# Cross-attention on one Trainium2 core: row maxima subtracted on VectorE, probabilities summed on GpSimd

## The chip, the cores and the metric

The kernel is one program on 1 core of a Trainium2 chip. The metric is the device time of that core in microseconds (us), from launch to the last result. Engines are named as the profile names them: PE is TensorE, DVE is VectorE, ACT is ScalarE, POOL is GpSimd, SP is SyncE. SBUF is the on-chip memory, PSUM the accumulators that PE writes.

## The reference

Three layers run one after the other: cross-attention, a mixer (attention on a quarter of the tokens, a state-space scan on the rest) and an expert layer. Only cross-attention is touched. Cut to it:

```python
def cross_attention(x1, x2, Wq1, Wk1, Wv1, Wk2, Wv2, Wo, bo):   # B=4, N1=256, N2=4096, D=256, 8 heads of 64
    q1, k1, v1 = heads(x1 @ Wq1), heads(x1 @ Wk1), heads(x1 @ Wv1)
    k2, v2 = heads(x2 @ Wk2), heads(x2 @ Wv2)
    k, v = concat([k1, k2], axis=1), concat([v1, v2], axis=1)    # 4352 keys
    sim = einsum('bihd,bjhd->bhij', q1, k) * 64 ** -0.5
    attn = softmax(sim, axis=-1)
    return einsum('bhij,bjhd->bihd', attn, v).reshape(B, N1, 512) @ Wo + bo
x = x + cross_attention(layernorm(x), ctx_1024, ...)
```

## The kernel before, in words

**Units, steps, tiles.** The work of cross-attention is cut into 16 units `u`: 4 batches, and in each 4 pairs of heads. A unit scores its 256 queries against 4352 keys, which are 17 tiles `j` of 256 keys (`HG` = 17), each for both heads of the pair: 128 partitions x 1024 numbers. The keys come in 9 groups `g` (`NG` = 9). A unit has 9 steps `d`: step `d` scores the tiles 2d and 2d+1, step 8 tile 16 alone.

**Two units at once.** While unit `u` makes its probabilities, the next one, `v` = u+1, projects its keys and finds the maxima of its rows. Each engine has its own program in a fixed order, written out by hand, and an instruction waits on counters (semaphores) of the others. In a step in the middle of a unit:

- PE (`block.tensor`): `score_for_max(v, d-1, 1)`, `score(u, 2d)`, `score(u, 2d+1)`, `score_for_max(v, d, 0)`, `project_keys(v, d+1)`, `weigh(u, 2d-2)`, then the projections of values that are due (`v_due`), `weigh(u, 2d-1)`.
- ACT (`block.scalar`): `exponentials(u, 2d)`, `exponentials(u, 2d+1)`, `store_k_hi(v, d+1)`, then `store_values` of what is due and pieces of the splitting of context and weights.
- DVE (`block.vector`): `reduce_max(v, d-1, 1)`, `add_probs(u, 2d-1)`, `reduce_max(v, d, 0)`, `add_probs(u, 2d)`, `split_keys(v, d+1)`.
- POOL (`block.gpsimd`): only the low halves of context and weights (`split_chunk`, `split_query_weights`, `split_weights`, `split_values_weights`).

Projections of values are due in odd units from step 2 on (two tiles a step) and in the steps 0 and 1 of even units (three tiles). The steps 2 to 7 of even units, and the steps 0 and 1 of odd units, have none: they are called light here. Others are called heavy.

**How a score becomes a probability.** `score` (L760 to L775) makes four products for each quarter tile, both heads in pairs that run side by side in the two halves of the array: three of them are q times k in high and low parts, the fourth (L774) adds the negated row maximum, as ones times `neg_max`. So the scores lie shifted in one of two slots of PSUM (`S`). `exponentials` (L460) takes them from PSUM to `probs` in SBUF, a ring of four tiles (`RING` = 4); that frees the slot, which `score` waits for. `add_probs` (L548) adds the tile to `prob_sum`, and `weigh` (L777) multiplies it with the values into the bank `O`. At the end of a unit `sum_probs` (L790) sums `prob_sum` over the partitions, `invert_sums` and `normalize` divide.

**The maxima.** `score_for_max` scores v with the high parts alone, into `M`, a single buffer of two banks; `reduce_max` (L534) takes the maxima of it, and the next `score_for_max` waits for that. At the end of a unit `reduce_rows` puts them into `max_cols`, `turn_maxima` (L745) turns them over the partitions on PE, and `store_neg_max` (L544) stores them; `score(v, 0)` waits for it.

**The keys.** `project_keys` fills the bank `KQ`; ACT rounds it to `k_hi` (`store_k_hi`, L446), then DVE takes what is left to `k_lo` (`split_keys`, L525), which waits for `k_hi_done`.

After the last unit, which has no unit beside it, the mixer begins once the output is added to `X1`.

Of the kernel before, what the change touches and what calls it, by code (L numbers as in the profile page):

```python
# [9 lines left out]
ALU = mybir.AluOpType  # L10
# [132 lines left out]
def cross_attention(nc, x, ctxT, w, X1, ident, psum):  # L143
# [3 lines left out]
    with ctx:  # L147
# [36 lines left out]
        maxes = sb("xa_maxes", [P, QT, 2, NG])  # L184

        max_cols = sb("xa_max_cols", [P, QT, P])
        neg_max = sb("xa_neg_max", [P, N1], F32R)
# [41 lines left out]
        neg_max_ready = sem("xa_neg_max_ready")  # L229
# [120 lines left out]
        def _(pool):  # L350
            pool.memset(ident[:, :], 0.0).then_inc(setup, 1)
            pool.memset(ones[:, :].bitcast(F32), 1.0).then_inc(setup, 1)
            pool.memset(max_cols[:, :, :], 0.0).then_inc(setup, 1)
            pool.wait_ge(setup, 3)
# [27 lines left out]

            split_query_weights(0)
# [24 lines left out]
        def _(act):  # L408
# [105 lines left out]
        def _(dve):  # L514
# [25 lines left out]
            def reduce_rows(v):  # L540
                dve.wait_ge(max_reduced, (v + 1) * NG * QT)
                dve.tensor_reduce(max_cols[:, :, 0:P:HD], maxes[:, :, :, :], AX_X, ALU.max).then_inc(rowmax_done, 1)
# [5 lines left out]
            def add_probs(u, j):  # L548
                n = u * HG + j
                dve.wait_ge(exp_done, n + 1)  # L550
                if j == 1:
                    if u > 0:
                        dve.wait_ge(sums_ready, u)
                    dve.tensor_tensor(prob_sum[:, :], probs[:, (n - 1) % RING, :], probs[:, n % RING, :],
                                      ALU.add).then_inc(summed, 1)
                else:
                    dve.wait_ge(summed, sums_done(n) - 1)
                    dve.tensor_tensor(prob_sum[:, :], prob_sum[:, :], probs[:, n % RING, :],  # L558
# [2153 lines left out]
```

## Time and profile before

| what | value |
|---|---|
| median of 3 runs | 1659.54 us (1658.64 to 1662.66) |
| profiled execution | 1661.31 us, with a span of 1659.3 us from its first to its last instruction |
| PE busy | 1489.4 us, 90% |
| DVE busy | 1124.6 us, 68% |
| ACT busy | 712.1 us, 43% |
| POOL busy | 443.8 us, 27% |
| cross-attention | from the start to about 1160 us |

Busy time is the time in which an engine executed at least one instruction. Matmuls overlap each other in PE's pipeline: the profile models their ends, so what a matmul occupies is read from the distance between two starts, not from its duration. In the timelines below a row is: start in us, duration in us, engine, line, operation, output<-inputs, shapes, count, and in brackets how long the engine sat idle before it and what ended that. Rows with a count over 1 are merged instructions. The clock (PEclk) is what was granted to TensorE, 1.00 being 2.4 GHz and 0.50 being 1.2 GHz.

### The profile page before, as it was taken

The page shows a single profiled execution, that of the slowest core. Times are in us where ns is not written, and L with a number is a line of the kernel's source. Part 1 is how long each engine was busy: PE and PEld are TensorE (multiplying, and loading weights), DVE is VectorE, ACT ScalarE, POOL GpSimd, SP SyncE. Part 2 cuts the span into 40 slices and gives each one's busy share as a digit, 9 for nine tenths or more (in the row PEclk, how much of TensorE's full clock was granted, in tenths as well). Part 3 has the DMA queues.
Part 4 walks back from the last instruction along what each step waited for, and adds up shares of the span by engine and source line. Part 5 has one row for each costly group of instructions (what it writes and reads, how often), then busy time and mean ns, then how long its engine had stood idle before and what let it go on. Part 6 is the DMA issues. An engine that isn't in the chain of part 4 may idle for free. (4 is left out here: it accounts for less than half of the span.)

```text
span 1659.3 us, 29603 instructions
## 1 busy us (share of the span) xinstructions
PE 1489.4 (90%) x11988; PEld 1121.4 (68%) x11988; DVE 1124.6 (68%) x1283; ACT 712.1 (43%) x971; POOL 443.8 (27%) x286
## 2 busy tenths in 40 slices
PE   4999999999999999999999999998597777827995
PEld 4877777776777777777777777766354444527995
DVE  2687578657657765865876685685676999644663
ACT  3443345443444543444454444333345333224773
POOL 4300003200000320100131000000133999433885
PEclk8999999999999999999999999999797999958998
DMA  5000021000002100000300000000304900092333
GB/s 174 14 11 11 1 84 51 1 14 11 11 15 87 36 2 14 20 1 27 99 11 2 23 11 2 2 1 1 84 10 178 231 0 0 1 362 63 63 59 58
DMA packets 62388, 76.50 MB, mean 46 GB/s; under 512 B 6385, under 2 KB 47985, under 8 KB 61857
## 3 DMA queue, kind: packets, MB, share of 16 engines
q1 hardware_dynamic: 57168, 68.51, 13.6%
q0 software_dynamic: 5088, 6.11, 2.5%
q8 instruction: 99, 1.62, 0.4%
q14 instruction: 33, 0.26, 0.1%
HBM read 58.39 MB, written 17.25 MB: 46 GB/s over the span
## 5 line engine op out<-in xcount | busy, mean ns | idle before, releaser
L537 DVE TENSOR_REDUCE xa_maxes<-psum 128x2 f32<-128x1024 f32 (+1 forms) x288 | 334.2, 1162 | 265.0 <-PE psum L741 264.9
L467 ACT ACTIVATE xa_probs<-psum 128x1024 f32<-128x1024 f32 x272 | 268.7, 1026 | 273.2 <-PE psum L774 272.8
L558 DVE TENSOR_TENSOR xa_prob_sum<-xa_prob_sum,xa_probs 128x1024 f32<-128x1024 f32 x240 | 313.1, 1305 | 11.3 <-ACT xa_probs L467 10.5
L786 PE MATMUL psum<-xa_probs,xa_vals 128*64 128x256 f32 x2176 | 280.5, 389 | 2.0 <-DVE xa_heads_T L572 1.5
L786 PEld LDWEIGHTS psum<-xa_probs,xa_vals 128*64 128x64 f32 x2176 | 139.4, 136 | 104.6 <-issue 41.8
L458 ACT ACTIVATE xa_vals<-psum 128x512 f32<-128x512 f32 x136 | 81.2, 597 | 207.6 <-PE psum L666 207.6
L768 PE MATMUL psum<-xa_q_hi,xa_k_hi 64*128 64x256 f32 x1088 | 156.4, 283 | 0.6 <-issue 0.6
L666 PE MATMUL psum<-xa_wv_hi,xa_ctx_hi 128*128 128x256 f32 x512 | 150.7, 294 | 4.4 <-DVE xa_maxes L537 4.4
L772 PE MATMUL psum<-xa_q_hi,xa_k_lo 64*128 64x256 f32 x1088 | 154.3, 279 | 0.0
L774 PE MATMUL psum<-xa_neg_max,xa_ones 64*128 64x256 f32 x1088 | 154.2, 279 | 0.0
L770 PE MATMUL psum<-xa_q_lo,xa_k_hi 64*128 64x256 f32 x1088 | 153.8, 278 | 0.0
L666 PE MATMUL psum<-xa_wv_lo,xa_ctx_hi 128*128 128x256 f32 x512 | 144.9, 283 | 0.0
L666 PE MATMUL psum<-xa_wv_hi,xa_ctx_lo 128*128 128x256 f32 x512 | 144.6, 283 | 0.0
L741 PE MATMUL psum<-xa_k_hi,xa_q_hi 64*128 64x512 f32 (+1 forms) x604 | 128.0, 430 | 15.2 <-DVE xa_maxes L537 8.7
L449 ACT ACTIVATE xa_k_hi<-psum 128x512 fp32r<-128x512 f32 (+1 forms) x151 | 83.0, 554 | 127.8 <-PE psum L666 127.8
L529 DVE TENSOR_TENSOR xa_k_lo<-psum,xa_k_hi 128x512 fp32r<-128x512 f32 (+1 forms) x151 | 94.5, 630 | 37.6 <-ACT xa_k_hi L449 37.3
L367 POOL TENSOR_TENSOR xa_w_lo<-xa_stage,xa_w_hi 128x512 fp32r<-128x512 f32 x16 | 20.5, 1282 | 371.9 <-ACT xa_w_hi L414 371.9
L361 POOL TENSOR_TENSOR xa_ctx_lo<-xa_ctx_in,xa_ctx_hi 128x1024 fp32r<-128x1024 f32 x32 | 79.6, 2491 | 145.8 <-ACT xa_ctx_hi L440 145.8
L666 PE MATMUL psum<-xa_ctx_hi,xa_w_hi 128*128 128x512 f32 x256 | 115.3, 450 | 2.5 <-issue 2.5
L666 PEld LDWEIGHTS psum<-xa_wv_hi,xa_ctx_hi 128*128 128x128 f32 x512 | 97.9, 191 | 27.3 <-issue 26.9
L1787 DVE TENSOR_TENSOR_SCAN mx_drive<-psum,mx_drive 128x768 f32<-128x768 f32 x64 | 110.0, 1743 | 7.8 <-POOL mx_drive L1312 6.9
L1312 POOL TENSOR_TENSOR mx_drive<-mx_xi,mx_rows 128x768 f32<-128x768 f32 x62 | 110.7, 1812 | 0.1
(329 smaller groups left out, 3019.5 us busy)
## 6 DMA issues: line engine op xcount, KB each, us to landing
xa_ctx_in<-in_ctxT_dram SPq DMA_DIRECT2D x32, 512.0 KB, 3.8
ex_slots<-mx_blank_tile SPq DMA_DIRECT2D x2, 4372.5 KB, 37.5
xa_stage<-in_L_xattn_Wk_dram SPq DMA_DIRECT2D x32, 128.0 KB, 2.4
xa_stage<-in_L_xattn_Wv_dram SPq DMA_DIRECT2D x16, 256.0 KB, 3.1
ex_raw<-in_L_ffn_w_gate_dram SPq DMA_DIRECT2D x8, 512.0 KB, 10.1
ex_raw<-in_L_ffn_w_up_dram SPq DMA_DIRECT2D x8, 512.0 KB, 10.8
ex_raw<-in_L_ffn_w_down_dram SPq DMA_DIRECT2D x8, 512.0 KB, 11.6
ex_xt<-ex_slots SPq DMA_DIRECT2D x15, 265.0 KB, 2.8
```

Of the source, the lines that this page charges most:

```text
L467: nc.scalar.activation(probs[:, n % RING, :], S[:, 2 * (n % 2):2 * (n % 2) + 2, :].rearrange("p h q -> p (h q)"), ACT.Exp, scale=HD ** -0. ...
L537: dve.tensor_reduce(maxes[:, qt, :, g:g + 1], max_banks(v, g, qt)[:, :, 0:group_keys(g)[1]], AX_X, ALU.max).then_inc(max_reduced, 1)
L558: dve.tensor_tensor(prob_sum[:, :], prob_sum[:, :], probs[:, n % RING, :], ALU.add).then_inc(summed, 1)
L666: i = pe.matmul(out, l, r, start=(c == 0 and k == 0), stop=(c == n - 1 and k == 2))
L741: i = pe.matmul(max_banks(v, g, qt)[:, h, part * N1:(part + slots) * N1], q_hi[half[h], v % 2, qt * P:(qt + 1) * P], k_hi[half[h], at:at + ...
L768: pe.matmul(out[h], k[h], q[h], start=True, stop=False)
L770: pe.matmul(out[h], k[h], q[2 + h], start=False, stop=False)
L772: pe.matmul(out[h], k[2 + h], q[h], start=False, stop=False)
L774: i = pe.matmul(out[h], ones[half[h], :], neg_max[half[h], :], start=False, stop=True)
L786: i = pe.matmul(O[half[h], 0:N1], vals[:, 2 * j + t, lanes:lanes + HD], probs[:, n % RING, (2 * h + t) * N1:(2 * h + t + 1) * N1], start=( ...
L1312: pool.tensor_tensor(drive[n % RINGS][:, :], dx[:, ct, :], b_rows[:, s, :], ALU.mult).then_inc(drive_done, 1)
L1787: dve.tensor_tensor_scan(drive[n % RINGS][:, :], decay[n % DECAYS], drive[n % RINGS][:, :], 0.0, ALU.mult, ALU.add).then_inc(scanned, 1)
```

## The change

The fourth product of `score` goes, and `neg_max` with it. The turned maxima are stored as they are, for both heads in all 128 partitions (`max_rows`, `store_max`), for which `turn_maxima` makes four turns of a broadcast column where it made two. DVE subtracts them from the scores on their way from PSUM to `probs` (`shift`), and that frees the slot of PSUM. ACT takes the exponential in place, from SBUF to SBUF, once `shifted` says so. `add_probs` is moved from DVE to POOL. The projection of the queries moves ahead of the last `weigh` of a unit. The order of ACT's program stays.

```diff
@@ block.gpsimd
+            def add_probs(u, j):
+                n = u * HG + j
+                pool.wait_ge(exp_done, n + 1)
+                if j == 1:
+                    if u > 0:
+                        pool.wait_ge(sums_ready, u)
+                    pool.tensor_tensor(prob_sum[:, :], probs[:, (n - 1) % RING, :], probs[:, n % RING, :],
+                                       ALU.add).then_inc(summed, 1)
+                else:
+                    pool.wait_ge(summed, sums_done(n) - 1)
+                    pool.tensor_tensor(prob_sum[:, :], prob_sum[:, :], probs[:, n % RING, :],
+                                       ALU.add).then_inc(summed, 1)
             for u, d in steps():
+                if d >= 1:
+                    add_probs(u, 2 * d - 1)
+                    add_probs(u, 2 * d)
@@ block.scalar
             def exponentials(u, j):
                 n = u * HG + j
-                if n >= RING:
-                    act.wait_ge(pv_done, n - RING + 1)
-                    act.wait_ge(summed, sums_done(n - RING))
-                act.wait_ge(scores_ready, n + 1)
-                nc.scalar.activation(probs[:, n % RING, :], S[:, 2 * (n % 2):2 * (n % 2) + 2, :].rearrange(
-                    "p h q -> p (h q)"), ACT.Exp, scale=HD ** -0.5).then_inc(exp_done, 1)
+                act.wait_ge(shifted, n + 1)
+                nc.scalar.activation(probs[:, n % RING, :], probs[:, n % RING, :], ACT.Exp,
+                                     scale=HD ** -0.5).then_inc(exp_done, 1)
@@ block.vector
-            def store_neg_max(v):
+            def store_max(v):
                 dve.wait_ge(max_turned, v + 1)
-                dve.tensor_scalar(neg_max[:, :], M[:, 1, 0:N1], -1.0, None, ALU.mult).then_inc(neg_max_ready, 1)
+                if v > 0:
+                    dve.wait_ge(shifted, v * HG)
+                dve.tensor_copy(max_rows[:, :, :].rearrange("p h q -> p (h q)"), M[:, 1, :]).then_inc(max_ready, 1)
+
+            def shift(u, j):
+
                 n = u * HG + j
+                dve.wait_ge(scores_ready, n + 1)
+                if j == 0:
+                    dve.wait_ge(max_ready, u + 1)
+                if n >= RING:
+                    dve.wait_ge(pv_done, n - RING + 1)
+                    dve.wait_ge(summed, sums_done(n - RING))
+                dve.tensor_tensor(probs[:, n % RING, :].rearrange("p (h t q) -> p h t q", h=2, t=2),
+                                  S[:, 2 * (n % 2):2 * (n % 2) + 2, :].rearrange("p h (t q) -> p h t q", t=2),
+                                  max_rows[:, :, :].unsqueeze(2).broadcast_to([P, 2, 2, N1]),
+                                  ALU.subtract).then_inc(shifted, 1)
@@ block.vector, the steps
-                if d >= 2 and not (d == STEPS - 1 and v < U):
-                    add_probs(u, 2 * d - 1)
+                shift(u, 2 * d)
                 if v < U:
                     reduce_max(v, d, 0)
                 if d < STEPS - 1:
-                    add_probs(u, 2 * d)
+                    shift(u, 2 * d + 1)
                     if v < U:
                         split_keys(v, d + 1)
@@ block.tensor
             def score(u, j):
                 n, g = u * HG + j, (j + 1) // 2
                 if n >= 2:
-                    pe.wait_ge(exp_done, n - 1)
-                if j == 0:
-                    pe.wait_ge(neg_max_ready, u + 1)
+                    pe.wait_ge(shifted, n - 1)
                     for h in range(2):
-                        pe.matmul(out[h], k[2 + h], q[h], start=False, stop=False)
-                    for h in range(2):
-                        i = pe.matmul(out[h], ones[half[h], :], neg_max[half[h], :], start=False, stop=True)
+                        i = pe.matmul(out[h], k[2 + h], q[h], start=False, stop=True)
                 i.then_inc(scores_ready, 1)
@@ block.tensor, turn_maxima
-                for qt in range(QT):
-                    i = pe.matmul(M[:, 1, qt * P:(qt + 1) * P], max_cols[:, qt, :], ident[:, :],
-                                  start=True, stop=True)
+                for h in range(2):
+                    for qt in range(QT):
+                        i = pe.matmul(M[:, 1, h * N1 + qt * P:h * N1 + (qt + 1) * P],
+                                      row_max[:, qt, h:h + 1].broadcast_to([P, P]), ident[:, :],
+                                      start=True, stop=True)
@@ block.tensor, step 8
+                    if u + 2 < U:
+                        project_queries(u + 2)
                     weigh(u, HG - 1)
...
-                    if u + 2 < U:
-                        project_queries(u + 2)
                     turn_maxima(v, values)
```

## Rows read from the trace of the kernel before

**Rows 1.** Windows: stretch, length, busy us (count) of each engine, PEclk, DMA.

```profile
137.00:1115.30 978.30, 963.70 (x8702) 728.17 (x8700) 676.14 (x682) 423.81 (x561) 101.22 (x56) 1.00 0.08 23
1115.30:1165.00 49.70, 39.62 (x440) 29.97 (x440) 28.03 (x27) 17.63 (x18) 0.82 (x5) 1.00 0.01 1
...
76.00:80.00 4.00, 3.43 (x18) 3.21 (x20) 1.66 (x5) 0.87 (x2) 4.00 (x7) 0.52 0.47 133
80.00:90.00 10.00, 9.01 (x80) 7.28 (x78) 4.80 (x6) 5.50 (x7) 1.60 (x3) 0.85 0.00 1
```

**Rows 2.** Timeline of DVE, one light step and the start of the next.

```profile
541.68 1.23 DVE L537 TENSOR_REDUCE xa_maxes<-psum 128x2 f32<-128x1024 f32 x1 [0.81 <-PE psum L741]
542.82 1.22 DVE L558 TENSOR_TENSOR xa_prob_sum<-xa_prob_sum,xa_probs 128x1024 f32<-128x1024 f32 x1
543.95 1.22 DVE L537 TENSOR_REDUCE xa_maxes<-psum 128x2 f32<-128x1024 f32 x1
...
546.22 0.68 DVE L529 TENSOR_TENSOR xa_k_lo<-psum,xa_k_hi 128x512 fp32r<-128x512 f32 x1
547.71 1.23 DVE L537 TENSOR_REDUCE xa_maxes<-psum 128x2 f32<-128x1024 f32 x1 [0.80 <-PE psum L741]
```

**Rows 3.** Timeline of PE, the first part of the same step.

```profile
541.13 0.50 PE L741 MATMUL psum<-xa_k_hi,xa_q_hi 64*128 64x512 f32 x2
541.47 0.28 PE L768 MATMUL psum<-xa_q_hi,xa_k_hi 64*128 64x256 f32 x2
...
541.95 0.28 PE L768 MATMUL psum<-xa_q_hi,xa_k_hi 64*128 64x256 f32 x2
...
543.38 0.39 PE L741 MATMUL psum<-xa_k_hi,xa_q_hi 64*128 64x512 f32 x2
```

**Rows 4.** Timeline of ACT, the same step.

```profile
542.71 1.97 ACT L467 ACTIVATE xa_probs<-psum 128x1024 f32<-128x1024 f32 x2 [2.23 <-PE psum L774]
545.39 0.60 ACT L449 ACTIVATE xa_k_hi<-psum 128x512 fp32r<-128x512 f32 x1 [0.70 <-PE psum L666]
```

**Rows 5.** PE waiting for DVE: timeline of a heavy step, and the view of waits.

```profile
598.44 1.21 DVE L537 TENSOR_REDUCE xa_maxes<-psum 128x2 f32<-128x1024 f32 x1
...
599.91 0.36 PE L666 MATMUL psum<-xa_wv_hi,xa_ctx_hi 128*128 128x256 f32 x1 [0.36 <-DVE xa_maxes L537]
...
PE psum L666 <- DVE xa_maxes L537: 4.4, 12, 0.4
```

**Rows 6.** Timeline around the start of an odd unit.

```profile
553.26 0.61 PE L752 MATMUL psum<-ident,xa_max_cols 128*128 128x128 f32 x4
...
553.90 0.42 DVE L546 TENSOR_SCALAR xa_neg_max<-psum 128x256 fp32r<-128x256 f32 x1 [0.91 <-PE psum L752]
...
561.57 1.74 DVE L563 RECIPROCAL xa_inv_sum<-psum 128x256 f32<-128x256 f32 x1
...
568.02 0.39 PE L741 MATMUL psum<-xa_k_hi,xa_q_hi 64*128 64x512 f32 x2
```

**Rows 7.** Timeline around the start of an even unit.

```profile
492.44 0.68 PE L752 MATMUL psum<-ident,xa_max_cols 128*128 128x128 f32 x4
...
511.55 1.23 DVE L537 TENSOR_REDUCE xa_maxes<-psum 128x2 f32<-128x1024 f32 x1 [2.12 <-PE psum L741]
```

**Rows 8.** Timeline of POOL and DVE where both work.

```profile
565.50 2.79 POOL L361 TENSOR_TENSOR xa_ctx_lo<-xa_ctx_in,xa_ctx_hi 128x1024 fp32r<-128x1024 f32 x1 [2.20 <-ACT xa_ctx_hi L440]
565.95 0.68 DVE L529 TENSOR_TENSOR xa_k_lo<-psum,xa_k_hi 128x512 fp32r<-128x512 f32 x1
567.68 1.69 DVE L558 TENSOR_TENSOR xa_prob_sum<-xa_prob_sum,xa_probs 128x1024 f32<-128x1024 f32 x1
```

**Rows 9.** Timeline of POOL alone, and of PE in the last unit.

```profile
58.69 4.76 POOL L361 TENSOR_TENSOR xa_ctx_lo<-xa_ctx_in,xa_ctx_hi 128x1024 fp32r<-128x1024 f32 x2
...
1114.55 0.71 PE L752 MATMUL psum<-ident,xa_max_cols 128*128 128x128 f32 x4 [0.54 <-DVE xa_max_cols L542]
...
1152.49 1.03 PE L795 MATMUL psum<-xa_prob_sum,xa_ones 128*64 128x256 f32 x8
```

More of the change, by code:

```diff
@@ L184, in cross_attention @@
         maxes = sb("xa_maxes", [P, QT, 2, NG])
-        max_cols = sb("xa_max_cols", [P, QT, P])
-        neg_max = sb("xa_neg_max", [P, N1], F32R)
+        row_max = sb("xa_row_max", [P, QT, 2])
+        max_rows = sb("xa_max_rows", [P, 2, N1])
         probs = sb("xa_probs", [P, RING, 2 * 2 * N1])
@@ L228, in cross_attention @@
         max_turned = sem("xa_max_turned")
-        neg_max_ready = sem("xa_neg_max_ready")
+        max_ready = sem("xa_max_ready")
+        shifted = sem("xa_shifted")
         scores_ready = sem("xa_scores_ready")
@@ L541, in reduce_rows @@
                 dve.wait_ge(max_reduced, (v + 1) * NG * QT)
-                dve.tensor_reduce(max_cols[:, :, 0:P:HD], maxes[:, :, :, :], AX_X, ALU.max).then_inc(rowmax_done, 1)
-            def store_neg_max(v):
+                dve.tensor_reduce(row_max[:, :, :], maxes[:, :, :, :], AX_X, ALU.max).then_inc(rowmax_done, 1)
+            def store_max(v):
                 dve.wait_ge(max_turned, v + 1)
-                dve.tensor_scalar(neg_max[:, :], M[:, 1, 0:N1], -1.0, None, ALU.mult).then_inc(neg_max_ready, 1)
-            def add_probs(u, j):
+                if v > 0:
+                    dve.wait_ge(shifted, v * HG)
+                dve.tensor_copy(max_rows[:, :, :].rearrange("p h q -> p (h q)"), M[:, 1, :]).then_inc(max_ready, 1)
+            def shift(u, j):
                 n = u * HG + j
[L550 to L558, printed above, removed]
-                                      ALU.add).then_inc(summed, 1)
+                dve.wait_ge(scores_ready, n + 1)
[8 more added lines that the diff above has]
+                                  ALU.subtract).then_inc(shifted, 1)
             def invert_sums(u):
@@ L597, in _ @@
             split_q(1)
-            store_neg_max(0)
+            store_max(0)
             for u, d in steps():
@@ L606, in _ @@
                             split_own(own_due(u, d))
-                    if u > 0:
-                        add_probs(u - 1, HG - 1)
+                    shift(u, 0)
                     if v < U:
                         reduce_max(v, 0, 0)
+                    shift(u, 1)
+                    if v < U:
                         split_keys(v, 1)
-                    add_probs(u, 1)
                     continue
@@ L631, in _ @@
                     reduce_rows(v)
-                    if u % 2 == 1:
-                        add_probs(u, 2 * d - 1)
-                    store_neg_max(v)
+                    store_max(v)
                     if u + 2 < U:
                         split_q(u + 2)
-                    if u % 2 == 0:
-                        add_probs(u, 2 * d - 1)
-            add_probs(U - 1, HG - 1)
             invert_sums(U - 1)
@@ L812, in _ @@
             turn_own(0)
-            pe.wait_ge(setup, 3)
+            pe.wait_ge(setup, 2)
             project_queries(0)
```

5 lines of the change are left out of this document (2 added, 3 removed).

## The prediction

> **What bounds the kernel now.** I read the windows first. Between 137 and 1115 us, units 1 to 14 and most of unit 0, PE is busy 963.7 of 978.3 us at the full clock, DVE 676.1, ACT 423.8, POOL 101.2 [rows 1]. So PE sets the pace there, and the timelines show with how much room. In a light step DVE's first `reduce_max` starts 6.03 us before the next one (541.68 to 547.71), and DVE sat idle 0.8 us in it, waiting for PE [rows 2]. That 0.8 us is all the distance between a step bounded by PE and one bounded by DVE. Heavy steps have some 3 us more of PE work and the same work on DVE and ACT. In the last unit PE has nothing beside the scores and the weighing and is busy 39.6 of 49.7 us [rows 1].
>
> One more thing is to be seen: the engines hand work to each other inside a step. `M` is one buffer, so `score_for_max`, `reduce_max`, `score_for_max` go in turn. And ACT is in order: `store_k_hi(v, d+1)` stands behind `exponentials(u, 2d+1)`. Now the exponentials follow PE: the two of a step are over at 544.68, while the keys come at 545.39 [rows 4]; nobody waits for that order.
>
> **Part 1: the fourth product goes.** Four pairs take 0.48 us (541.47 to 541.95), so one pair takes 0.12 us [rows 3]. Two pairs fewer for each of 17 x 16 = 272 tiles: 544 x 0.12 = 65 us off PE, 0.48 us a step. `turn_maxima` has 8 records in place of 4, at 0.11 us each (0.61 us for four, of which the last takes 0.28) [rows 6]: +0.43 us, 16 times, 7 us back. If nothing else bound, that would be 58 us.
>
> **Part 2: what the gain runs into on M.** `score_for_max(v, d-1, 1)` starts at 541.13, its `reduce_max` 0.55 us later and takes 1.23 us [rows 2, 3]. PE then needs 0.26 us to start: a reduction ends at 599.65 and the product that waited for it starts at 599.91 [rows 5]. So the second `score_for_max` can't start before 0.55 + 1.23 + 0.26 = 2.04 us; it now starts at 2.25 (543.38) [rows 3]. Only 0.21 of the 0.48 us are to be had in any step where PE is otherwise the bound.
>
> **Part 3: DVE's work is exchanged, not reduced.** 256 adds go. An add holds DVE 1.13 us up to the next instruction (542.82 to 543.95) [rows 2]. 272 shifts come. None is in the trace. The nearest row is `split_keys`, which reads PSUM and SBUF too: 512 numbers in 0.68 us, where an add and a reduction of 1024 take 1.22 and 1.23 [rows 2]. Twice `split_keys` is 1.36 us as a ceiling, with its fixed part counted twice; one reduction less 0.1 us, for a port that might be quicker, is a floor. I take 1.22 us, 1.14 to the next. The waits of a shift (up to four) cost nothing in the rows where ACT has three. `store_max` copies 512 numbers in place of 256, +0.27 us, 16 times, in the path from one unit to the next.
>
> **Part 4: the new wait, and what is queued behind it.** The shift stands between PE and the exponential. DVE's order is R1 (`reduce_max(v, d-1, 1)`), shift 2d, R0, shift 2d+1, `split_keys(v, d+1)`. The last waits for `k_hi(d+1)`, which ACT does only after `exponentials(u, 2d+1)`, which waits for shift 2d+1. So DVE, right behind that shift, stands idle through a whole exponential and a store of keys, in every step. Behind `split_keys` is queued the next R1, for which PE waits. Counted from R1: three operations at 1.14 = 3.41, shift 2d+1 to its end 1.22, to ACT 0.05 (estimate; ACT to DVE is a few hundredths, between nothing and the 0.26 us of PE), exponential to the next instruction 0.95 (two in 1.97) [rows 4], keys 0.60 [rows 4], to DVE 0.03, `split_keys` 0.60 (0.68 with the overlap seen in rows 2). Sum 6.86 us. A light step takes 6.03 now: **+0.83 us**, bounded by the circle DVE, ACT, DVE. An exponential from SBUF isn't in the trace; I take that from PSUM, with 0.9 and 1.2 us as ends. Light steps 2 to 7 of 8 even units are 48; three of them contain `project_output` and DVE's wait for it, in which the circle runs hidden, so 45 x 0.83 = **+37 us**.
>
> In heavy steps PE needs about 9.2 us and the circle is hidden: each gains the 0.21 us of part 2. The 12 waits of 0.36 us for R0, where an add was held up [rows 5], go too. An odd unit gets 5 x 0.21, a share of these 4.4 us (0.6) and the 0.24 us of tile 16: -1.9 us, 7 units, **-13 us**.
>
> **Part 5: the starts of units.** An odd unit starts with light steps and also with the reciprocal. From the start of `turn_maxima`, now: second `score_for_max` of step 2 at 568.02 - 553.26 = 14.76 us [rows 6]. After: `store_max` starts at 1.07 (0.64 now, + 0.43), ends 1.67; low queries and keys to 2.55; shift 0 when its scores are there, 2.6 to 3.75; short reduction 4.35; shift 1 ends 5.57; ACT's exponential and keys until 7.2; split 7.8; short reduction 8.4; reciprocal 1.78 and product 0.35 [rows 6] 10.5; shift 2 11.7; R0 12.8; shift 3 ends 14.0; ACT 15.65; split 16.25; R1 ends 17.5; PE 17.75. That is +3.0 us, 7 times: **+21 us**. An even unit starts with heavy steps: the first long R1 now comes at 511.55 - 492.44 = 19.1 us [rows 7]; PE's own work to there shrinks by 0.96 - 0.43, but the reciprocal and one circle follow PE's last piece, so I take -0.4, 7 times; unit 0 without values to project, +0.9; the ends of even units -0.2, 8 times: **-3.5 us**.
>
> **Part 6: POOL.** Two subtractions of 1024 from SBUF to SBUF take 4.76 us with nothing beside them, 2.38 each [rows 9]; the one that shares time with DVE's adds took 2.79 [rows 8]. An add has the same shape. With the wait of each add for the one before it I take 2.5 us, with 2.35 and 2.8 as ends. Two in a light step of 6.9 us leave room, also where a `split_chunk` of 2.4 us joins them (four tiles of ring absorb that). What is queued behind the adds on POOL are the weight and context splits, which are due a step or more later; SP's loads wait on them, and are as far ahead. The cover is gone in the last unit: PE alone would need 3.5 us a step, POOL needs 5. Now `sum_probs` comes 1152.49 - 1114.55 = 37.9 us after the turn [rows 9]. After: two shifts and an exponential until 5.3, the first add until 7.7, fifteen more at 2.5 and 0.26 to PE: 45.5. **+7.6 us** (5 to 12). After it the mixer and the experts are untouched.
>
> DVE's adds were held up by POOL: one took 1.69 us where others take 1.22, ending with POOL's instruction, while `split_keys` in the same 2.79 us took its 0.68 [rows 8]. The shift reads one input from SBUF, as `split_keys` does, so I expect no such wait.
> The Trainium skill (SBUF — State Buffer, section Who interferes with whom) says the same: a DVE instruction with two SBUF inputs contends with a GpSimd instruction that reads SBUF, one with a single SBUF input doesn't. By that rule the trace agrees, and these holds vanish. Against the change speaks another of its rules (GPSIMD Engine Reference, Performance versus the Vector engine): a GpSimd add of two fp32 inputs takes 1.96 times the Vector engine's, 4497 ns for 2048 numbers. An estimate from it for 1024 is 2.25 us, which would make the last unit +4 us.
>
> **The sum.** 37 - 13 + 21 - 3.5 + 7.6 = +49 us on the profiled 1661.3 us: 1710.5. The profiled execution lies 1.8 us above the median; on the median it is 1709. I say 1710.
>
> **The rivals.**
> *A, faster: PE stays the bound.* If the keys were stored early enough, or DVE's wait for them lay outside the circle, a light step would take 5.81 us (6.03 - 0.22). This decides from the point where the circle is shorter than 5.8 us, 1.05 us less than my sum. For it speaks that PE is 98% busy; against it the fixed order of ACT's program, which the change leaves. 45 x -0.22 = -10, odd starts 0, -13, -3.5, +7.6: -19 us, 1641. 11%.
> *B: the clock falls.* PE gets a pause of about 1.3 us in each light step, and 2.7 us in each odd start ahead of 17.75. After a pause of 1.55 us near 76 us the clock was 0.52 and then 0.85 [rows 1], which cost 4 x 0.48 + 10 x 0.15 = 3.4 us; but the last unit ran 80% busy at 1.00 [rows 1]. If each of 7 odd starts paid it: +24 us, 1734. 15%.
> *C: POOL is the bound.* It decides from 3.4 us an add. At 4 us a light step takes 8: +50 us on 45 of them and +22 us in the last unit, 1783. Speaking for it are only the 2.79 us in rows 8. 5%.
> *D: the shift shares the port with POOL after all,* and is held 0.5 us each time as the add was [rows 8]: 1 us a light step, 2 an odd start, +59 us, 1770. The 0.68 us speak against it. 4%.
> *E: errors cancel,* the circle about 6 us long: within 0.3%. 3%.
>
> **How the numbers follow.** My own forecast has 62%. Its size hangs on the circle, +/-0.25 us in 45 steps and twice in each odd start (+/-15 us), and on the last unit (-2 to +4): 1693 to 1728. The range reaches over B, 1688 to 1748, and leaves out A, C, D, E and a little: about 2 in 10. About 0.3% is what a measurement of this kernel can tell from no change. Faster 0.11 (A), same 0.03 (E), slower 0.86 (the rest).
>
> **What the profile after would show.** Part 4: R1 to R1 in a light step 6.86 us, DVE idle before `split_keys` 1.6 to 1.7 us with `k_hi` as its releaser, ACT's exponential released by DVE. Part 2: second `score_for_max` of a heavy step 2.04 us after the first. Part 3: shifts at 1.22 us. Part 5: 17.75 us from the turn in odd units. Part 6: adds on POOL every 2.5 us in the last unit, `sum_probs` 45.5 us after the turn. The forecast is wrong if `split_keys` doesn't wait for ACT, if shift or add miss their ends, or if the windows show a clock below 1.00.

## The result and the profile after

| what | before | after |
|---|---|---|
| median | 1659.9 us (4 runs, 1658.64 to 1662.66) | 1736.32 us (4 runs, 1731.98 to 1737.56) |
| profiled execution | 1661.31 us | 1735.36 us |
| ratio after / before | | 1.0453, 95% interval 1.0430 to 1.0477 |

The change makes the kernel 4.5% slower: +76 us on the medians, +74 us between the profiled executions, where +49 was forecast. The page after: busy time of each engine, POOL and the granted clock in 40 slices, four groups of instructions (busy us, mean ns of one | idle us before them, releaser); behind them the window from 3.1 us after the first turn of unit 1 to 0.8 us after the last one, as in rows 1 (columns as there). It holds units 1 to 14 alone (unit 0 is over at 133.9 us before and at 136.6 after), and it is 62 us longer than that of before although PE does less in it.

```profile
PE 1470.3 (85%) x10964; PEld 1079.7 (62%) x10964; DVE 1128.5 (65%) x1299; ACT 713.1 (41%) x971; POOL 1048.4 (60%) x541
...
POOL 3375557747546774744678375467403999723885
PEclk8999999999999999999999999999589999967998
...
L393 POOL TENSOR_TENSOR xa_prob_sum<-xa_prob_sum,xa_probs 128x1024 f32<-128x1024 f32 x240 | 572.1, 2384 | 261.9 <-ACT xa_probs L480 244.4
L480 ACT ACTIVATE xa_probs<-xa_probs 128x1024 f32<-128x1024 f32 x272 | 288.1, 1059 | 556.6 <-DVE xa_probs L572 556.4
...
L572 DVE TENSOR_TENSOR xa_probs<-psum,xa_max_rows 128x1024 f32<-128x1024 f32 x272 | 330.1, 1215 | 14.6 <-POOL xa_prob_sum L393 9.0
...
L542 DVE TENSOR_TENSOR xa_k_lo<-psum,xa_k_hi 128x512 fp32r<-128x512 f32 (+1 forms) x151 | 95.8, 638 | 208.6 <-ACT xa_k_hi L465 206.8
```

```profile
139.64:1180.33 1040.69, 949.34 (x7814) 694.84 (x7811) 679.26 (x696) 423.83 (x561) 629.57 (x280) 0.99 0.07 21
```

The last group of the page is the finding in one line: 151 splits of keys take 96 us, and DVE sat idle 208.6 us in front of them, 206.8 of these waiting for `k_hi` from ACT. DVE is busy as long as it was (1128.5 us, 1124.6 before); its work now stands at the wrong place.

The light step that answers to rows 2 and 4 (timelines of DVE and of ACT after):

```profile
564.04 1.22 DVE L550 TENSOR_REDUCE xa_maxes<-psum 128x2 f32<-128x1024 f32 x1
565.17 1.22 DVE L572 TENSOR_TENSOR xa_probs<-psum,xa_max_rows 128x1024 f32<-128x1024 f32 x1
566.30 1.22 DVE L550 TENSOR_REDUCE xa_maxes<-psum 128x2 f32<-128x1024 f32 x1
567.44 1.22 DVE L572 TENSOR_TENSOR xa_probs<-psum,xa_max_rows 128x1024 f32<-128x1024 f32 x1
570.26 0.69 DVE L542 TENSOR_TENSOR xa_k_lo<-psum,xa_k_hi 128x512 fp32r<-128x512 f32 x1 [1.61 <-ACT xa_k_hi L465]
570.87 1.22 DVE L550 TENSOR_REDUCE xa_maxes<-psum 128x2 f32<-128x1024 f32 x1
```

```profile
568.68 1.06 ACT L480 ACTIVATE xa_probs<-xa_probs 128x1024 f32<-128x1024 f32 x1 [1.20 <-DVE xa_probs L572]
569.65 0.58 ACT L465 ACTIVATE xa_k_hi<-psum 128x512 fp32r<-128x512 f32 x1
```

Follow the circle: R1 at 564.04, shift, R0, shift until 568.66; ACT's exponential at 568.68; keys at 569.65 until 570.23; split at 570.26; R1 at 570.87. Apart from the overlap of neighbouring instructions every one of them waits for the one before. The step takes 6.83 us (6.03 before).

Where the 74 us came in, by the distances between the starts of `turn_maxima` (us):

| stretch | before | after | difference |
|---|---|---|---|
| unit 0, turn to turn | 57.4 | 60.8 | +3.4 |
| 7 odd units, 1 to 13 | 545.0 | 571.1 | +26.1 |
| 7 even units, 2 to 14 | 435.6 | 471.9 | +36.3 |
| last unit, turn to `sum_probs` | 37.9 | 46.8 | +8.9 |
| all else | | | -0.8 |

### The profile page after: what moved, and what is told of

Its sections match the earlier page's. It is cut to its first block and busy times, and to the rows that moved or that the text cites. A ratio compares the mean times of both kernels' runs of the same rounds, so it can differ in the third digit from the quotient of the medians.

```text
span 1733.2 us, 27857 instructions
## 1 busy us (share of the span) xinstructions
PE 1470.3 (85%) x10964; PEld 1079.7 (62%) x10964; DVE 1128.5 (65%) x1299; ACT 713.1 (41%) x971; POOL 1048.4 (60%) x541
## 5 line engine op out<-in xcount | busy, mean ns | idle before, releaser
L393 POOL TENSOR_TENSOR xa_prob_sum<-xa_prob_sum,xa_probs 128x1024 f32<-128x1024 f32 x240 | 572.1, 2384 | 261.9 <-ACT xa_probs L480 244.4
L480 ACT ACTIVATE xa_probs<-xa_probs 128x1024 f32<-128x1024 f32 x272 | 288.1, 1059 | 556.6 <-DVE xa_probs L572 556.4
L572 DVE TENSOR_TENSOR xa_probs<-psum,xa_max_rows 128x1024 f32<-128x1024 f32 x272 | 330.1, 1215 | 14.6 <-POOL xa_prob_sum L393 9.0
L793 PE MATMUL psum<-xa_probs,xa_vals 128*64 128x256 f32 x2176 | 285.1, 393 | 4.5 <-ACT xa_probs L480 3.0
L542 DVE TENSOR_TENSOR xa_k_lo<-psum,xa_k_hi 128x512 fp32r<-128x512 f32 (+1 forms) x151 | 95.8, 638 | 208.6 <-ACT xa_k_hi L465 206.8
L750 PE MATMUL psum<-xa_k_hi,xa_q_hi 64*128 64x512 f32 (+1 forms) x604 | 137.4, 456 | 84.1 <-issue 66.3
L793 PEld LDWEIGHTS psum<-xa_probs,xa_vals 128*64 128x64 f32 x2176 | 140.1, 138 | 109.7 <-issue 46.8
L750 PEld LDWEIGHTS psum<-xa_k_hi,xa_q_hi 64*128 64x128 f32 x604 | 59.1, 185 | 157.2 <-issue 144.1
L777 PEld LDWEIGHTS psum<-xa_q_hi,xa_k_hi 64*128 64x128 f32 x1088 | 105.5, 186 | 9.4 <-DVE xa_probs L572 6.0
```

The source lines that it names most:

```text
L393: pool.tensor_tensor(prob_sum[:, :], prob_sum[:, :], probs[:, n % RING, :], ALU.add).then_inc(summed, 1)
L480: nc.scalar.activation(probs[:, n % RING, :], probs[:, n % RING, :], ACT.Exp, scale=HD ** -0.5).then_inc(exp_done, 1)
L572: dve.tensor_tensor(probs[:, n % RING, :].rearrange("p (h t q) -> p h t q", h=2, t=2), S[:, 2 * (n % 2):2 * (n % 2) + 2, :].rearrange("p h ...
L750: i = pe.matmul(max_banks(v, g, qt)[:, h, part * N1:(part + slots) * N1], q_hi[half[h], v % 2, qt * P:(qt + 1) * P], k_hi[half[h], at:at + ...
L777: pe.matmul(out[h], k[h], q[h], start=True, stop=False)
L793: i = pe.matmul(O[half[h], 0:N1], vals[:, 2 * j + t, lanes:lanes + HD], probs[:, n % RING, (2 * h + t) * N1:(2 * h + t + 1) * N1], start=( ...
```

## The experiments

Each was measured against the kernel before on the same chip. "The step" is the distance from one R1 to the next. R1 and R0 are the names of the prediction: `reduce_max(v, d-1, 1)` and `reduce_max(v, d, 0)`; the reductions of group 0 are short (512 numbers), all others long (1024).

**1. The circle cut on ACT.** The changed kernel, with the keys stored between the two exponentials of a step.

```diff
@@ block.scalar, the steps
-                for j in step_tiles(d):
+                for j in step_tiles(d)[:1]:
                     exponentials(u, j)
                 if d + 1 < NG and v < U:
                     store_k_hi(v, d + 1)
+                for j in step_tiles(d)[1:]:
+                    exponentials(u, j)
```

> The changed kernel, with one move in ACT's program: store_k_hi(v, d+1) stands between the two exponentials of a step and no longer behind both. Nothing else differs. Theory 1 (the circle DVE, ACT, DVE through the second exponential and the keys is the bound of light steps): split_keys finds its keys ready, a light step falls from 6.83 us to 5.8 us, 45 x 1.0 = 46 us less; the seven odd starts lose 3 us each of circle and their pause of PE (with it the half clock of some 1.5 us), about 31 us less. Sum 1736 - 77 = about 1659 us. Rival 1 (POOL's adds are the bound, 2.4 us each, with the ring of four tiles behind them): the order on ACT changes nothing, 1736 us. Rival 2 (the clock, lowered by PE's pauses, is most of the loss, and the circle isn't): between 1715 and 1736 us.

Measured: 1661.03 us beside 1659.14, ratio 1.0009 (0.9999 to 1.0020). DVE, then PE, in a light step:

```profile
529.38 1.23 DVE L552 TENSOR_REDUCE xa_maxes<-psum 128x2 f32<-128x1024 f32 x1 [0.56 <-PE psum L752]
...
532.78 1.22 DVE L574 TENSOR_TENSOR xa_probs<-psum,xa_max_rows 128x1024 f32<-128x1024 f32 x1
533.91 0.68 DVE L544 TENSOR_TENSOR xa_k_lo<-psum,xa_k_hi 128x512 fp32r<-128x512 f32 x1
535.15 1.23 DVE L552 TENSOR_REDUCE xa_maxes<-psum 128x2 f32<-128x1024 f32 x1 [0.56 <-PE psum L752]
```

```profile
528.83 0.51 PE L752 MATMUL psum<-xa_k_hi,xa_q_hi 64*128 64x512 f32 x2
...
530.48 0.28 PE L783 MATMUL psum<-xa_q_hi,xa_k_lo 64*128 64x256 f32 x2
530.71 0.49 PE L752 MATMUL psum<-xa_k_hi,xa_q_hi 64*128 64x512 f32 x2
531.13 0.50 PE L677 MATMUL psum<-xa_ctx_hi,xa_w_hi 128*128 128x512 f32 x1
```

The split starts right behind the shift, R1 waits for PE again, and the step is 5.77 us. Another order of the same calls on ACT gives back 75 us: all that the change lost. It sums up from the steps: 45 light ones x 1.06 = 48, the odd starts 16.4 to 13.3 us = 22, the falls of the clock behind them 10, even starts 3.5, less some 9 in units 3, 7 and 11 where POOL comes later still (experiment 5). Yet the kernel only stands where it stood. Its steps are shorter than before (5.77 us for 6.03, 8.98 for 9.24, and 12 heavy ones 8.98 for 9.64), 26 us together; but the last unit takes 8.9 us more than before, the starts of units 3, 7 and 11 take 12 more, the starts of even units 5.5 and the ends of odd ones 4.8.

**2. The queries back at the end.** The changed kernel, `project_queries` again behind the last values and just ahead of `turn_maxima`.

> The changed kernel, with the projection of the queries put back behind the due values at the end of a unit, as in the kernel before. Theory (at the ends of odd units turn_maxima waits 0.78 us for ACT to store the last values, which the projection of the queries used to cover): the seven odd ends fall from 9.3 us to 8.4 us, measured from the last but one long R1 to the turn, together 6 us less, 1730 us; even ends, which have no values, 0 to 0.7 us more each because the turn then follows the projection, up to 5 us back. Rival (the end of odd units waits for the reduction of the maxima on DVE): no change, 1736 us.

Measured: 1724.85 us beside 1659.14, ratio 1.0401 (1.0384 to 1.0419); 11.5 us less than the changed kernel. The turn after and here (timelines of PE and ACT), then the view of waits after, from 137 to 1180 us (total us, times, longest):

```profile
516.21 1.13 PE L762 MATMUL psum<-ident,xa_row_max 128*128 128x128 f32 x8 [0.78 <-ACT xa_vals L474]
...
515.47 0.60 ACT L474 ACTIVATE xa_vals<-psum 128x512 f32<-128x512 f32 x1 [0.84 <-PE psum L675]
...
PE psum L675 <- DVE xa_maxes L550: 7.7, 7, 1.1
...
PE psum L762 <- ACT xa_vals L474: 5.5, 7, 0.8
```

```profile
513.28 1.13 PE L762 MATMUL psum<-ident,xa_row_max 128*128 128x128 f32 x8
```

The wait of 0.78 us is gone, and an odd end (last long R1 but one to the turn) goes from 9.32 to 8.43 us (8.64 before); an even end loses 0.21 (but for unit 14, which has no queries to project). That makes 7 x 0.89 - 6 x 0.21 = 5.0 us in units 1 to 14, and 0.1 us at each of their seven odd starts; more the edit isn't shown to give. Of the 10.2 us between the two profiled spans the rest lies where it changes nothing: 2.7 behind cross-attention, 1.6 in the falls of the clock in step 2 and 1.3 in one at the start of unit 3 (both below), against 1.2 more in unit 0.

**3. Only the fourth product left out.** The kernel before without L773 and L774. It leaves out the subtraction of the row maximum.

> The kernel before, without the fourth product of score: the row maximum is found, turned and stored as before but not added to the scores, so the exponentials are taken of unshifted scores. It measures what the product is worth by itself. Theory (in steps bounded by PE the single buffer M lets the second score_for_max start no sooner than 2.04 us after the first, so that only 0.21 of 0.48 us are gained): light steps 5.8 us in place of 6.03, heavy ones 0.2 us less; 15 x (7 x 0.21 + 0.48 + 0.24) = 33 us and 4 us in the last unit: 1660 - 37 = 1623 us. Rival (PE alone bounds, each pair saved counts): 1660 - 65 = 1595 us.

Measured: 1626.98 us beside 1659.14, ratio 0.9809 (0.9793 to 0.9825). A heavy step in it (PE):

```profile
570.74 0.50 PE L741 MATMUL psum<-xa_k_hi,xa_q_hi 64*128 64x512 f32 x2
...
572.61 0.50 PE L741 MATMUL psum<-xa_k_hi,xa_q_hi 64*128 64x256 f32 x4
```

So 32 us is what the product costs in this order of work, of the 65 us that PE spends on it. Light steps go from 6.03 to 5.77, heavy ones from 9.24 to 8.98: 0.26 us each, of 0.48. In e1 the 0.48 can be followed. The second `score_for_max` comes 530.71 - 528.83 = 1.88 us after the first, where it came at 2.25 [rows 3]: 0.37 won. It can't come earlier, as R0's buffer is read until 529.38 + 1.23 = 530.61. The next products follow at 0.42 us (530.71 to 531.13) instead of 0.31 (543.38 to 543.69 in the step of rows 3): 0.11 given back.

**4. Only the sums moved.** The kernel before, `add_probs` on POOL instead of DVE.

> The kernel before with add_probs moved from DVE to POOL, at the same place of POOL's program as in the changed kernel; the four products and the exponentials from PSUM stay. Theory (POOL keeps up in all steps that have a unit beside them, since two adds of 2.45 us fit into 6.03 us, and the last unit is bounded by it): light steps stay 6.03 us, the last unit takes 45 to 47 us from the turn to sum_probs in place of 37.9, +8 us; the 12 held values of 0.36 us go, -4 us; 1660 + 4 = 1664 us, up to 1670 where the splits on POOL delay the sums at two or three unit boundaries. Rival (POOL's adds or a shared port are the main loss of the change): 1690 to 1736 us.

Measured: 1659.22 us, ratio 1.0005 (0.9995 to 1.0015). POOL in the last unit, and PE's wait for it:

```profile
1114.22 37.50 POOL L393 TENSOR_TENSOR xa_prob_sum<-xa_prob_sum,xa_probs 128x1024 f32<-128x1024 f32 x15
...
PE psum L786 <- POOL xa_prob_sum L393: 7.7, 1, 7.7
```

Fifteen adds in 37.50 us, 2.50 each; the last unit takes 44.8 us instead of 37.9. The same amount comes back elsewhere, 7.2 us of it in the odd units and 1.1 in unit 0. Light steps stay at 6.03. The heavy steps of 9.64 us in units 3, 7, 11, where adds of DVE were held beside POOL, become 9.24. The first long R1 of an odd unit comes 12.5 us after the turn instead of 13.3 (13.1 in units 3, 7, 11), of which step 2 takes 0.2 back. The move is worth nothing either way.

**5. POOL's backlog at the start of units 3, 7, 11.** e1, with the first two of a batch's splits of context in steps 2 and 5 of the unit two ahead of it, where they were in its steps 7 and 8.

```diff
-            at = (u % PAIRS - 2) * STEPS + d - 7
-            return at if u + 2 < U and 0 <= at < CHUNKS else None
+            if u + 2 >= U or u % PAIRS < 2:
+                return None
+            if u % PAIRS == 2:
+                return {2: 0, 5: 1}.get(d)
+            return d + 2 if d + 2 < CHUNKS else None
```

> As e1_keys_between, and in every fourth unit (u = 2, 6, 10) the splits of the next batch's context chunks 0 and 1 stand in the steps 2 and 5, where they stood in 7 and 8. Theory (at three boundaries the sums of POOL are late because two chunk splits and two weight splits are crowded into the last three steps: sum_probs comes 7.9 to 9.1 us after the turn there and 6.2 or 5.1 elsewhere, and the first long R1 of the next unit 2.7 to 5.1 us later than in other odd units): those three starts become like the others, 10 to 12 us less, 1650 us. Rival (these starts are late for the loads of context or weights, not for POOL's adds): no change, 1661 us.

Measured: 1659.1 us, ratio 1.0000 (0.9988 to 1.0011), 2 us below e1 (measured on another chip), where 10 to 12 less were expected. POOL in unit 2:

```profile
243.34 10.00 POOL L396 TENSOR_TENSOR xa_prob_sum<-xa_prob_sum,xa_probs 128x1024 f32<-128x1024 f32 x4
253.28 2.40 POOL L364 TENSOR_TENSOR xa_ctx_lo<-xa_ctx_in,xa_ctx_hi 128x1024 fp32r<-128x1024 f32 x1
...
260.52 1.29 POOL L370 TENSOR_TENSOR xa_w_lo<-xa_stage,xa_w_hi 128x512 fp32r<-128x512 f32 x1
```

POOL has no idle time here, with the splits moved too: with steps of 5.77 us, two adds of 2.5 leave 0.77 us a step, and each split (2.40, 1.29) costs more. The first R1 of units 3, 7, 11 comes at 8.4 to 10.0 us after the turn, where it came at 9.3 to 11.7 in e1 and at 6.6 in other odd units. So POOL is the cause, but not by the sums that were expected. At the start of unit 7 (turn at 545.54), POOL and PE:

```profile
550.14 0.74 POOL L376 TENSOR_TENSOR xa_w_lo<-xa_stage,xa_w_hi 128x256 fp32r<-128x256 f32 x1
...
550.98 0.47 PE L680 MATMUL psum<-xa_ctx_hi,xa_w_hi 128*128 128x512 f32 x1 [1.82 <-issue]
```

PE has been idle for 1.82 us when it starts `project_keys(v, 1)`, 0.10 us after `split_weights` on POOL has ended (550.88), for which that product waits; `sum_probs` only follows behind the keys. In other odd units that split is over 1.8 us after the turn (1.5 in the changed kernel); here it stands right behind adds that keep POOL busy until 550.19. The profile names no releaser; that it is this split rests on the program's order and on the 0.10 us, which return in units 3, 7 and 11 of the changed kernel and of e1, e5, e6, e7, e9 and e10. Moving two context splits brought the product from 6.3 to 5.4 us after the turn. The rest of the scatter is TensorE's clock: behind this pause it falls in units 7 and 11 of e1 and of e5 (0.50 from 553 to 557 us in e1, 0.62 from 551 to 555 in e5) and in unit 3 of neither. No run moved `split_weights` itself ahead of the adds.

**6. The last unit shared in two blocks.** e1; in unit 15 POOL sums tiles up to 8, DVE the rest.

> As e1_keys_between, and in the last unit POOL adds the tiles up to 8, DVE the tiles 9 to 16, each three tiles behind its shift. Theory (in the last unit POOL's adds are the bound, DVE is free there): from the turn to sum_probs some 38 us in place of 46.8, 1661 - 9 = 1652 us. Rival (the latency from shift over exponential to weighing bounds the last unit): 1659 to 1661 us.

Measured: 1655.72 us, ratio 0.9980 (0.9970 to 0.9989). The last unit takes 43.2 us, not 46.8, where 38 was expected: the ring of four lets nobody run ahead, so POOL sets 2.5 us a tile in the first half, and in the second DVE sets 2.49 with a shift and an add a tile.

**7. Queries last, splits early and shared sums together.**

> e1_keys_between with the early chunks of e5_chunks_early, the shared sums of e6_last_sums_shared and the projection of the queries behind the due values, as in e2_queries_last. If the causes are separate places of the timeline, the gains add: 1661 - 11 - 9 - 6 = 1635 us, and the kernel is faster than both. If they hide each other, between 1640 and 1650 us.

Measured: 1650.9 us, ratio 0.9952 (0.9935 to 0.9968). By the medians the three parts gave 1.9 (e5 against e1), 5.3 (e6 against e1) and, by its steps, some 5 us (e2) alone, 12 together; here they give 10.1. So they add up nearly, and each was less than hoped: 1635 us is missed by 16.

**8. Is it `M` that holds the 0.22 us?** e7, in steps 3 to 7 of even units with `project_keys` ahead of the second `score_for_max`, so that nothing waits for `M`.

```diff
@@ block.tensor
-                    score_for_max(v, d, 0, values)
+                    if not light(u, d):
+                        score_for_max(v, d, 0, values)
...
                     project_keys(v, d + 1, maxima, values)
+                    if light(u, d):
+                        score_for_max(v, d, 0, values)
```

> As e7_all_three, and in the light steps 3 to 7 of even units PE projects the keys ahead of the second score_for_max, and DVE does both shifts ahead of its R0. It tests the single buffer M as the bound of those steps: PE's own work is 5.55 us, the steps now take 5.77. Theory: 5.55 us, 40 x 0.22 = 9 us less than e7_all_three. Rival (DVE, 5.15 us busy, with its waits becomes the bound in its place): no gain, or some us more than e7_all_three.

Measured: 1649.28 us, ratio 0.9934 (0.9911 to 0.9957): no gain over e7. Windows of even unit 6 in it:

```profile
500.00:530.00 30.00, 30.00 (x260) 21.11 (x261) 26.32 (x26) 16.20 (x20) 26.50 (x12) 1.00 0.31 93
```

The step stays at 5.76 us, with PE busy 30.00 of 30 us, as it is in e7. The second `score_for_max`, which waits for nobody here, still takes 0.43 us up to the next product, and 0.08 us stand between scores and keys. So PE itself needs 5.76 us in this order too; whether `M` or the change from one kind of product to another takes the rest can't be told apart by it.

**9. The last unit shared tile by tile.** As e7, but in unit 15 POOL adds the odd tiles and DVE the even ones, in turn.

```diff
@@ block.gpsimd
                     add_probs(u, 2 * d - 1)
-                    add_probs(u, 2 * d)
+                    if u < U - 1:
+                        add_probs(u, 2 * d)
@@ block.vector
                 shift(u, 2 * d)
+                if v == U and d > 1:
+                    add_last(2 * d - 2)
```

> As e7_all_three, but in the last unit POOL adds the odd tiles and DVE the even ones, in turn. In e7_all_three the last unit stayed at 43.2 us from the turn to sum_probs, for two reasons that its trace shows: POOL's adds every 2.5 us hold the ring, and then DVE needs 2.49 us for a shift and an add. In turn, an add on each engine makes 2.5 + 1.3 = 3.8 us for two tiles, DVE has 3.5 us of work for two, PE 3.5. Theory: 5 + 8 x 3.8 + 1.3 = 37 us from the turn to sum_probs, 6 us less: 1651 - 6 = 1645 us. Rival (handing the sum from engine to engine and the ring together cost what is gained): 1650 us.

Measured: 1640.08 us (1639.28 to 1640.09) beside 1657.77, ratio 0.9888 (0.9871 to 0.9904). It beats both kernels. DVE and POOL in the last unit:

```profile
1115.59 1.23 DVE L587 TENSOR_TENSOR xa_prob_sum<-xa_prob_sum,xa_probs 128x1024 f32<-128x1024 f32 x1 [0.37 <-POOL xa_prob_sum L396]
...
1119.46 1.23 DVE L587 TENSOR_TENSOR xa_prob_sum<-xa_prob_sum,xa_probs 128x1024 f32<-128x1024 f32 x1 [0.29 <-POOL xa_prob_sum L396]
...
1116.96 2.39 POOL L396 TENSOR_TENSOR xa_prob_sum<-xa_prob_sum,xa_probs 128x1024 f32<-128x1024 f32 x1 [1.48 <-DVE xa_prob_sum L587]
```

Two tiles take 3.87 us (1115.59 to 1119.46), against 5.0 with POOL alone, and `sum_probs` comes 39.3 us after the turn, where 37 was expected. The gain of this edit over e7 is those 3.9 us (39.3 for 43.2). So the median of 1640 us is below the 1645 of the theory by luck, not by the edit. The other 6 us between the two profiled spans lie where it changes nothing: 4.9 behind cross-attention, for which no cause is shown, and 2.8 in unit 0, where e7 runs at a clock of 0.55 from 76 to 83 us and e9 at 1.00, less 1.4 in unit 3, where e9 has a fall of the clock (0.75 from 268 to 272 us) and e7 none. Beside the kernel before, the profiled execution is 21 us shorter, all of it ahead of the last turn (1114.6 to 1093.0 us); the low clock near 76 us, which the prediction priced at 3.4 us [rows 1] and e9 doesn't have, is part of that.

**10. The circle cut on DVE instead.** The changed kernel; `split_keys` moved behind the first reduction of the next step, ACT's order left.

```diff
@@ block.vector
                     reduce_max(v, d - 1, 1)
+                    split_keys(v, d)
...
                     shift(u, 2 * d + 1)
-                    if v < U:
-                        split_keys(v, d + 1)
```

> The changed kernel with ACT's order as it is, and one move on DVE: split_keys(v, d+1) stands behind the first reduce_max of the next step, no longer right behind the second shift. It cuts the circle at its other end. Theory (the loss in light steps is the circle, wherever it is cut): light steps 5.8 to 6.0 us, the odd starts lose their pause, 1660 to 1672 us. Rival (what e1_keys_between gained came from ACT storing the keys earlier, for PE's sake, and DVE's place in it doesn't matter): 1720 us or more.

Measured: 1688.49 us, ratio 1.0182 (1.0165 to 1.0199), above what was expected. DVE in a light step, and the view of waits:

```profile
546.89 1.23 DVE L550 TENSOR_REDUCE xa_maxes<-psum 128x2 f32<-128x1024 f32 x1 [0.65 <-PE psum L747]
...
552.75 1.23 DVE L550 TENSOR_REDUCE xa_maxes<-psum 128x2 f32<-128x1024 f32 x1 [0.65 <-PE psum L747]
...
PEld psum L672 <- DVE xa_k_lo L542: 33.6, 94, 0.5
```

The circle is cut here as well: the step is 5.86 to 5.88 us with ACT untouched. But PE now waits for `k_lo`, 94 times. Against e1 each light step is 0.11 us longer and each heavy one 0.12, step 2 of an odd unit 0.7 and step 1 of an even one 1.1. By units that is 13.2 us in the odd ones, 13.0 in the even ones and 1.1 in unit 0, the whole 27 us between the medians of e10 and e1; which part of it is the wait for `k_lo` (33.6 us in all, some of it hidden) and which the longer queue of DVE wasn't separated. Cut at DVE the circle moves its wait to PE; ACT was the place with room.

## Why the prediction was right and where it was wrong

**Part 4, the circle: right.** Forecast 6.86 us, measured 6.83; DVE's idle time 1.6 to 1.7 us, measured 1.61 with `k_hi` as releaser. 45 x 0.80 = 36 us for 37. e1 and e10 show it by cutting it at two places. Each piece was within 0.05 us of its row: the exponential from SBUF takes 1.06 us, where one from PSUM takes 1.03 (means of 272), and 0.97 to the next instruction, where 0.95 was taken.

**Part 1 and 2: the size was right, the place wrong.** The floor was put at 2.04 us between the two `score_for_max`; it is 1.88, as PE starts 0.10 us after the reduction ends and not 0.26. The row from which the 0.26 came shows a product of values [rows 5]. 0.37 us were to be had there and 0.11 lost just behind, so the step gains 0.26 where 0.21 was said. Heavy steps take 8.98 us after.

**Part 3: right.** The shift takes 1.22 us, 1.13 to the next. This is its row after, in units 1 to 14 (ns, least/median/most; first and last start):

```profile
L572 DVE TENSOR_TENSOR xa_probs<-psum,xa_max_rows x238: 1210/1214/1225, 139.4 to 1175.8; 128x1024 f32<-128x1024 f32 x119
```

Its longest is 1.23 us with POOL busy 60% of that stretch, so it is never held. The add of rows 8 took 1.69 us, and of the 240 adds in the kernel before 29 took over 1.4 and the longest 2.52. Rival D is out. One reading was wrong: the add of rows 8 doesn't end with POOL's instruction (568.29) but at 569.37, 1.08 us behind it, so it looks held until POOL was through and then run. By the rule of the Trainium skill that the prediction names (SBUF — State Buffer, section Who interferes with whom), the trace agrees.

**Part 5, odd starts: right in length, and it brought rival B with it.** PE's turn, the second `score_for_max` of step 2, and two windows (columns as in rows 1) after:

```profile
435.03 1.16 PE L762 MATMUL psum<-ident,xa_row_max 128*128 128x128 f32 x8
...
452.76 0.50 PE L750 MATMUL psum<-xa_k_hi,xa_q_hi 64*128 64x512 f32 x2 [2.50 <-issue]
```

```profile
449.00:453.00 4.00, 1.50 (x22) 1.19 (x18) 2.39 (x4) 1.54 (x2) 3.86 (x2) 1.00 0.00 0
454.00:458.00 4.00, 4.00 (x18) 2.27 (x17) 2.33 (x3) 2.48 (x4) 2.90 (x2) 0.62 0.00 0
```

452.76 - 435.03 = 17.73 us, forecast 17.75. PE had stood idle for 2.50 of the 4 us ahead (1.50 busy); then the clock falls to the lower of its two levels for some 3 us, and step 2 takes 10.5 us instead of 9.0 (11.7 in unit 7). Six of seven odd starts have it, 10 us together. The rival had named place and cause and priced 3.4 us each, 24 together; my own sum held it at nothing, though the pause of 2.7 us was in the prediction and a clock below 1.00 was named as a sign that the forecast is wrong. The fall isn't certain: in e2, unit 5 has the same pause and none:

```profile
448.00:453.00 5.00, 2.50 (x29) 1.99 (x27) 3.39 (x4) 1.54 (x2) 4.38 (x2) 1.00 0.00 0
453.00:457.00 4.00, 4.00 (x28) 2.93 (x27) 2.56 (x3) 2.46 (x4) 2.39 (x2) 1.00 0.00 0
```

With the circle cut (e1) the pause shrinks to 0.8 us and these falls go: each odd step 2 takes 8.98 us. Other falls stand at the starts of units 3, 7 and 11 (Part 6).

**Part 5, even starts: the step that failed.** Forecast -0.4 us each, measured +1.1 to +1.4, 7 times: about 12 us. "PE's own work to there shrinks" was right and worthless. In the waits shown with e2, PE stands 1.1 us for R0 seven times, in front of a product of values: R0 of step 1, which had the reciprocal alone ahead of it, now has a shift too, and comes 3.86 us behind R1 instead of 2.73. I had counted the queue of DVE through the start of an odd unit and not through that of an even one.

**The moved projection: the step that is missing.** The prediction lists the move of `project_queries` in the change and prices it nowhere; it gave odd ends the gain of tile 16 (-0.24). They lost 0.68 us (8.64 to 9.32). The queries had covered ACT's store of the last values, for which `turn_maxima` waits. Against the forecast that is 7 x (0.68 + 0.24) = 6.4 us; e2 gives the wait back. The step cost nothing of its own, but it was the cover of a wait of 0.8 us.

**Part 6, POOL: the last unit right, low by 1.3 us; what is queued behind the adds wrong.** The last unit after (PE's turn, POOL, PE's `sum_probs`):

```profile
1179.58 1.16 PE L762 MATMUL psum<-ident,xa_row_max 128*128 128x128 f32 x8 [0.32 <-DVE xa_row_max L555]
...
1185.21 2.36 POOL L389 TENSOR_TENSOR xa_prob_sum<-xa_probs 128x1024 f32<-128x1024 f32 x1 [4.66 <-ACT xa_probs L480]
1188.46 2.39 POOL L393 TENSOR_TENSOR xa_prob_sum<-xa_prob_sum,xa_probs 128x1024 f32<-128x1024 f32 x1 [0.89 <-ACT xa_probs L480]
1191.28 35.03 POOL L393 TENSOR_TENSOR xa_prob_sum<-xa_prob_sum,xa_probs 128x1024 f32<-128x1024 f32 x14 [0.43 <-POOL xa_prob_sum L393]
...
1226.37 1.98 PE L802 MATMUL psum<-xa_prob_sum,xa_ones 128*64 128x256 f32 x8 [5.54 <-POOL xa_prob_sum L393]
```

Fourteen adds in 35.03 us are the 2.5 us that were taken; the first waits 0.3 us longer, and the second waits 0.89 us for its probabilities. The estimate of 2.25 us for an add was half of the 4497 ns that the Trainium skill (GPSIMD Engine Reference, Performance versus the Vector engine) gives for 2048 numbers; measured are 2.38. Its ratio of 1.96 fits better: the same add takes 1.22 us on DVE [rows 2], and 2.38 is 1.95 times that.

The prediction said of the splits behind the adds that they are due a step or more later. That step fails at three starts. In units 3, 7 and 11, where context splits join the adds, `split_weights` comes last in POOL's queue and the next product of keys waits for it. Unit 7 after (turn at 582.82):

```profile
587.61 0.72 POOL L373 TENSOR_TENSOR xa_w_lo<-xa_stage,xa_w_hi 128x256 fp32r<-128x256 f32 x1
...
588.43 0.47 PE L675 MATMUL psum<-xa_ctx_hi,xa_w_hi 128*128 128x512 f32 x1 [2.00 <-issue]
```

PE stands idle for 2.0 us there, and `sum_probs`, behind it in PE's order, comes 7.1 to 7.3 us after the turn instead of 5.2. The pause is partly hidden: units 7 and 11 start 0.6 us late. Unit 3 starts 2.0 us late, as the clock falls behind the pause (0.85 and 0.72 in the 4 us each from 287 and 291 us). That is 3 us together here, and 12 in e1, where the split ends later still.

**The sum.** Forecast 49. To that: falls of the clock in step 2 +10, even starts +12, odd ends +6.4, the weights behind POOL's adds +3 (1.3 of it the clock), last unit +1.3; against it the heavy steps (0.26 for 0.21), even ends (-0.44 for -0.2), unit 0 (+3.4 for +5.7), the light steps (0.80 for 0.83) and 0.8 us outside, -8 together. That gives 74, as measured. The three that matter lie at the starts and ends of units, where DVE's queue and ACT's lead over PE were looked at once and not for both kinds of unit. The measured time is that of rival B (1734) and lies outside my own 1693 to 1728; it is inside the stated range because that range reached over B. In part this is luck: the falls of the clock gave some 12 of B's 24 us, and the rest came from even starts, odd ends and the last unit, for which the range had not been widened.

## What to carry to other kernels

When an operation is put between two engines, follow the new chain through every in-order queue it enters and see whether it comes back to where it began: here the order of two calls in ACT's program decided 75 us, with no change in any engine's work. Do that for each kind of start and end, not for the middle alone, and ask of work that only moves what it was covering. Ask the same of work that is given to an idle engine: what is queued behind it, and who waits for that at a boundary? And count on a saving at the bottleneck only as far as its buffers let it through: of 0.48 us less on TensorE in a step 0.26 arrived.

## What the runs showed that I had not expected

- After a pause of 2.5 us the clock of TensorE fell in six of seven odd starts of the changed kernel, and not in the seventh; in e2, with the same pauses, it stayed at full speed in one more of them. A fall cost 1.4 to 2.7 us. Shorter pauses could do it too: after one of 1.8 us it fell in units 7 and 11 of e5 and not in unit 3, and after one of 2.0 us in unit 3 of the changed kernel and not in units 7 and 11. Which of two equal places falls no run here explains.
- The second `score_for_max`, when it had waited, starts 0.10 us after the reduction it waited for ended (a product of values took 0.26 [rows 5]), and the next ones follow 0.11 us later than without a wait (0.42 for 0.31 us), so a short wait costs more than it shows as idle time. Changing from one kind of product to another without a wait cost about as much in e8; why it didn't cost that in the kernel before stays open.
- Adds on GpSimd, each waiting for the one before, come every 2.50 us at 2.39 each; handed back and forth between GpSimd and VectorE, two of them take 3.87 us (2.39 + 1.23 + 0.25 for two hand-overs), so the chain across two engines is quicker than GpSimd's own (5.0 us). VectorE could do the two adds in less than 2.5 us, but in the last unit it has the shifts as well (2.49 us for a shift and an add in e6).
